# Expert stage of a gated cross-attention block on one core: the next chunk's transpose a unit later, routing squeezed into eight units, and the shared unit written straight to its place

## The reference, cut to what matters

```python
x = x + tanh(g_xattn) * xattn(layernorm(x), ctx, Wq, Wk, Wv, Wo, bo)
h = layernorm(x)
logits = h @ gate_w.T
scores = sigmoid(logits)
choice = scores + bias                     # 4 groups of 8 experts
best two groups by the sum of their best two choices
best 8 experts in these groups; weight = 2.5 * score / sum of the 8 scores
final = sum over experts of weight * down(silu(gate(h)) * up(h))
x = x + tanh(g_ffn) * (final + shared_down(silu(shared_gate(h)) * shared_up(h)))
```

## Time and profile before

| | us |
|---|---|
| median of 3 runs | 726.13 |
| lowest, highest | 724.36, 729.16 |
| the profiled execution, its own time | 733.6 |
| its span, from first to last instruction | 731.8 |
| expert stage in it, from 410 to the end | 322 |
| mean granted TensorE clock | 0.971 |

### The profile page before, as it was taken

How to read it: one execution, slowest core, us unless ns; L and a number is a source line. 1 busy time by engine, 2 the same in 40 slices (tenths; PEclk the granted TensorE clock), 3 DMA queues, 4 the chain that set the end, 5 groups by cost and what they waited for, 6 DMA issues and landing times.

```text
span 731.8 us, 16937 instructions
## 1 busy us (share of the span) xinstructions
PE 701.1 (96%) x4696; PEld 593.8 (81%) x4696; DVE 529.2 (72%) x1646; ACT 333.3 (46%) x626; POOL 268.8 (37%) x317
## 2 busy tenths in 40 slices
PE   8699999999999999999998989999899998999996
PEld 5589898898989889898887867878687786878784
DVE  5556776777767777777746497878778794969663
ACT  3224343343434334443443445556555554555553
POOL 4021212212122121221300165656656563756654
PEclk9859999999999999999997899999999999999999
DMA  5300001000000000000000544435352535454460
GB/s 141 107 19 19 20 20 24 17 17 17 18 23 17 18 17 19 21 17 20 15 2 1 130 105 99 122 95 127 94 140 75 145 100 122 126 119 129 99 150 15
DMA packets 44797, 47.22 MB, mean 65 GB/s; under 512 B 11728, under 2 KB 27216, under 8 KB 44752
## 3 DMA queue, kind: packets, MB, share of 16 engines
q1 hardware_dynamic: 44752, 46.72, 26.0%
HBM read 43.81 MB, written 2.62 MB: 63 GB/s over the span
## 4 chain that ended last, share of the span: by engine, by line
PE 81%; issue 8%; DVE 6%; POOL 3%; DMA 1%; DVEq 1%; POOLq 0%; ACT 0%; SPq 0%; ACTq 0%
PE bank L1052 16%; PE bank L977 11%; PE bank L979 11%; PE bank L978 11%; PE bank L1085 8%; PE bank L1012 5%; PE bank L1060 5%; POOL halves L446 3%; PE bank L1032 3%; PE bank L1038 2%; PE bank L1041 2%; PE bank L1035 2%; PE bank L984 1%; DVE xn L668 1%; PE bank L1022 1%
## 5 line engine op out<-in xcount | busy, mean ns | idle before, releaser
L446 POOL TENSOR_TENSOR halves<-area,halves 128x512 fp32r<-128x512 f32 x136 | 177.0, 1302 | 161.9 <-ACT halves L565 160.9
L522 ACT ACTIVATE area<-bank 128x512 f32<-128x512 f32 x128 | 69.5, 594 | 192.0 <-PE bank L1041 192.0
L937 DVE TENSOR_TENSOR bank<-area,bank 128x512 f32<-128x512 f32 x136 | 93.7, 689 | 62.0 <-PE bank L979 47.9
L1052 PE MATMUL bank<-ctx_keys,area 128*128 128x65 f32 x1024 | 130.1, 281 | 0.0
L1052 PEld LDWEIGHTS bank<-ctx_keys,area 128*128 128x128 f32 x1024 | 127.8, 201 | 0.7 <-issue 0.7
L575 ACT ACTIVATE area<-bank 128x512 f32<-128x512 f32 x136 | 81.3, 598 | 100.7 <-PE bank L979 100.1
L977 PE MATMUL bank<-x2t_hi,w_hi 128*128 128x512 f32 x272 | 110.7, 407 | 3.3 <-DVE area L948 2.4
L979 PE MATMUL bank<-x2t_lo,w_hi 128*128 128x512 f32 x272 | 106.7, 392 | 0.0
L978 PE MATMUL bank<-x2t_hi,w_lo 128*128 128x512 f32 x272 | 106.5, 392 | 0.0
L688 DVE TENSOR_REDUCE row_max<-bank 128x4 f32<-128x512 f32 x128 | 82.2, 684 | 33.5 <-PE bank L1012 32.4
L394 POOL TENSOR_TENSOR ctx_hi<-ctx_raw,ones_col 128x128 fp32r<-128x128 f32 x32 | 12.8, 401 | 253.0 <-PE bank L1041 244.2
(11 more groups left out here) (118 smaller groups left out, 1132.9 us busy)
## 6 DMA issues: line engine op xcount, KB each, us to landing
wbc<-rows_dram SPq DMA_DIRECT2D x128, 256.0 KB, 4.3
w_raw<-experts SPq DMA_DIRECT2D x32, 102.0 KB, 2.0
ctx_raw<-ctx_t SPq DMA_DIRECT2D x64, 32.0 KB, 2.1
out<-area SPq DMA_DIRECT2D x8, 256.0 KB, 3.8
ctx_keys<-ctx_nat SPq DMA_DIRECT2D x32, 32.0 KB, 1.8
max_rows<-max_t SPq DMA_DIRECT2D x64, 4.0 KB
area<-wq_t SPq DMA_DIRECT2D x1, 512.0 KB, 4.2
area<-wo SPq DMA_DIRECT2D x1, 512.0 KB, 4.9
```

The source lines that it names most:

```text
L446: nc.gpsimd.tensor_tensor(hid_lo[:, u % SLOTS, :], hid[:, u % HIDS, :], raw(hid_hi[:, u % SLOTS, :]), ALU.subtract).then_inc(hidlo_ready, 1)
L522: nc.scalar.activation(probs_t[:, k, :, :], st_ps[q][:].rearrange("p (h n) -> p h n", h=4), ACT.Exp)\
L937: nc.vector.tensor_tensor(up_ps[u % UPS][:], silu_g[:, u % 2, :], up_ps[u % UPS][:], ALU.mult)\
L1052: ins = nc.tensor.matmul(u_ps[q][:, i * (CD + 1):(i + 1) * (CD + 1)], probs_t[:, k, i, :], ctx_keys[:, b, :], start=True, stop=True)
```

## The change

Six edits, all in the expert stage:

1. PE: the transposes of chunk c+1 move from behind unit 0 to behind unit 1; the router product moves from behind unit 2 to behind unit 3.
2. ACT: `x2t_out` moves from unit 1 to unit 2, with `x2t_high` right behind it. The Tanh of the logits moves to unit 4, the Silu to unit 5.
3. DVE: step 0 moves from unit 3 to unit 4. Steps 1 to 20 now take 16 places, from place 1 of unit 5 to place 0 of unit 13, where they took 20 places.
4. ACT: `weights_out` moves to the top of unit 15, ahead of that unit's Silu.
5. DVE: in unit 0 `gate_up` writes its product straight into `hid`, and the copy at line 944 goes. For that it now waits until POOL has done the low half of the unit that last used this slot (unit 15 of the chunk before).
6. The counts of the semaphore `gated_ready` are adapted (16 in a chunk, where there were 17).

```diff
-ROUTE_FROM, ROUTE_TO = 4, 14
+ROUTE_FROM, ROUTE_PLACES = 2 * 5 + 1, 16
...
+        def gated_before(c, u):
+            return (UNITS - 1) * c + (u - 2 if u > 0 else 0)
...
             def experts_of(c, parity, first, last):          # ACT
                 for u in range(UNITS):
+                    if u == WEIGHTS_AT + 1 and not last:
+                        weights_out(c + 1)
                     act.wait_ge(gate_done, UNITS * c + u + 1)
-                    wait(act, gated_ready, free_of(2, c, u))
+                    if u == 2:
+                        act.wait_ge(hid_ready, UNITS * c + 1)
+                    else:
+                        wait(act, gated_ready, gated_before(c, u))
...
-                        if u == 1:
+                        if u == 2:
                             x2t_out(c + 1)
-                        if u == 2:
                             x2t_high(c + 1, 1 - parity)
-                        if u == 3:
-                            sigmoids(c + 1)
-                        if u == WEIGHTS_AT + 1:
-                            weights_out(c + 1)
+                        if u == 4:
+                            sigmoid_high(c + 1)
+                        if u == 5:
+                            sigmoid_low(c + 1)
...
-                if u == 3 and place == 1:                    # DVE, levels_at
+                if u == 4 and place == 1:
                     route_levels[0](c + 1)
-                at, places, levels = 2 * (u - ROUTE_FROM) + place, 2 * (ROUTE_TO - ROUTE_FROM), len(route_levels) - 1
+                at, places, levels = 2 * u + place - ROUTE_FROM, ROUTE_PLACES, len(route_levels) - 1
...
-                nc.vector.tensor_tensor(up_ps[u % UPS][:], silu_g[:, u % 2, :], up_ps[u % UPS][:], ALU.mult)\
-                    .then_inc(gated_ready, 1)
+                if u == 0:
+                    wait(dve, hidlo_ready, free_of(HIDS, c, u))
+                    nc.vector.tensor_tensor(hid[:, u % HIDS, :], silu_g[:, u % 2, :], up_ps[u % UPS][:], ALU.mult)\
+                        .then_inc(hid_ready, 1)
+                else:
+                    nc.vector.tensor_tensor(up_ps[u % UPS][:], silu_g[:, u % 2, :], up_ps[u % UPS][:], ALU.mult)\
+                        .then_inc(gated_ready, 1)
...
-                    if u > 0:
+                    if u > 1:
                         weigh_hidden(c, u - 1)
...
-                    if u == 0 and not last:                  # PE
+                    if u == 1 and not last:
                         if not first:
                             pe.wait_ge(wt_ready, c + 1)
                         transpose_norm(NCH + c + 1, misc_ps)
-                    if u == 2 and not last:
+                    if u == 3 and not last:
                         if not first:
                             pe.wait_ge(weight_ready, c + 1)
                         route(c + 1, route_ps)
```

More of the change, by code:

```diff
@@ L490, in x2t_high, with sigmoid_high, sigmoid_low @@
                 nc.scalar.activation(x2t_hi[:, parity, :], x2t[:], ACT.Copy).then_inc(x2hi_ready, 1)
-            def sigmoids(c, ps=route_ps):
+            def sigmoid_high(c, ps=route_ps):
                 act.wait_ge(logits_done, c + 1)
                 nc.scalar.activation(tanh_half[:], ps[:, 0:CB * NE], ACT.Tanh, scale=0.5).then_inc(sig_ready, 1)
+            def sigmoid_low(c, ps=route_ps):
                 act.wait_ge(route_step, ROUTE_STEPS * c + 1)
@@ L545, in attention @@
                     if last and b == 2:
-                        sigmoids(0, scores_ps[1])
+                        sigmoid_high(0, scores_ps[1])
+                        sigmoid_low(0, scores_ps[1])
                     if not (first and b == 0):
@@ L936, in gate_up @@
                 dve.wait_ge(up_done, n + 1)
-                nc.vector.tensor_tensor(up_ps[u % UPS][:], silu_g[:, u % 2, :], up_ps[u % UPS][:], ALU.mult)\
-                    .then_inc(gated_ready, 1)
+                if u == 0:
[5 more added lines that the diff above has]
+                        .then_inc(gated_ready, 1)
             def weigh_hidden(c, u):
-                dve.wait_ge(gated_ready, UNITS * c + u + 1)
+                dve.wait_ge(gated_ready, (UNITS - 1) * c + u)
                 wait(dve, hidlo_ready, free_of(HIDS, c, u))
[L943 to L950, removed]
+                group, i = divmod(u - 1, 2)
+                dve.wait_ge(wbc_in[group % WBC_SLOTS], 32 * (WBC_GROUPS // WBC_SLOTS * c + group // WBC_SLOTS + 1))
+                nc.vector.tensor_tensor(hid[:, u % HIDS, :], up_ps[u % UPS][:], wbc[:, group % WBC_SLOTS, i, :],
+                                        ALU.mult).then_inc(hid_ready, 1)
             def experts_of(c, parity, first, last):
```

## The result

| | before | after |
|---|---|---|
| median | 727.64 (4 runs) | 749.12 (4 runs, 747.78 to 751.75) |
| ratio | | 1.0272, 95% interval 1.0212 to 1.0332 |
| profiled execution, span | 731.8 | 750.0 |
| start of the expert stage (first gate matmul) | 410.07 | 412.28 |
| expert stage, from there to the end | 321.7 | 337.7 |

A forecast was written before the change was run, and what follows sets the result against it. PE, busy 96%, was taken as the bound, with DVE just keeping pace. Terms -7.5 + 11.4 - 0.3 = +3.6 us, less 0.8 for the slow stretch, gave +2.8 on the median 726.13: 728.9, range 718 to 733.

The forecast's parts named there:

- The wait on the normalised chunk: PE's 8.0 us of waits for the next chunk's normalised tiles, chunks 1 to 6; claimed to go, 7.5 us saved net.
- step 2: Routing step on DVE, now in place 0: held behind POOL's low half from 4.76 until 5.93, missing by 0.16 us.
- step 10: Routing copy on DVE: comes at 13.1 while POOL runs from 12.9 to 14.2, so it is held, missing by 0.2 us.
- the sum: DVE and POOL queues added up from unit 5: 1.9 us lost per plain chunk, 11.4 in chunks 1 to 6; total +3.6.
- Step 3's 0.71 us: Routing step on DVE after unit 5's `weigh_hidden`: claimed to meet POOL's `x2t_low` (5.9 to 7.2) and end at 7.28.
- the wait at unit 9: First of PE's waits on `weigh_hidden` claimed before units 9 to 11 in every chunk: 0.28 us of 1.2 a chunk.
- From here the steps are small.: DVE's routing steps after the third added-up wait: claimed to take 0.08 to 0.65 us, so that DVE stays level.
- Step 12: Routing step on DVE that makes the groups' mask: taken at 0.08 us, among the steps assumed small.
- 0.6 us come back there: Chunks 3 and 5: unit 1's up product waits 0.6 us for the old chunk's last `weigh_hidden`, leaving 1.6 saved in each.
- half of it, -0.8: Slow-clock stretch of 1.7 us after chunk 5's idle time: may go with that idle time, so half was counted, -0.8.
- The third one, slower: Rival: step 2 is held by both POOL operations, 2.4 us instead of 1.2; 11 us in all, 737; chance 0.12.
- the first one: Rival: DVE's queue absorbs the denser steps, never more than 1.85 us back; 717 to 718.6; chance 0.20.

The follow-up runs named there:

- packing alone: The kernel before with only the places of the twenty routing steps changed, to 16 places from place 1 of unit 5: ratio 1.0251, median 753.16.
- early copy alone: The kernel before with only the copy of the weights moved to the top of unit 15: ratio 1.0031.
- step 2 from the bank: The changed kernel with routing step 2 reading the logits' bank (PSUM) instead of the SBUF tile: ratio to the kernel before 1.0126.
- copy kept: The changed kernel without the straight product, the shared unit again going through its bank and the copy at line 944: ratio to the kernel before 1.0113.
- step 12 from the bank: The changed kernel with routing step 12, the groups' mask, reading the logits' bank instead of the SBUF tile: ratio to the kernel before 1.0094.
- 18 places: The changed kernel with the twenty routing steps in 18 places, from place 0 of unit 5, instead of 16: ratio to the kernel before 1.0033.
- bank reads: The changed kernel with seven routing steps reading one operand from the logits' bank instead of an SBUF tile: ratio to the kernel before 0.9887, median 724.88.

## Why the prediction was wrong

**Right in kind.** The wait on the normalised chunk went, and VectorE's queue took its place, with steps held behind POOL's subtractions; step 2 and step 10 were held as the sum said, in place 0, by margins of 0.1 to 0.3 us. Step 3's 0.71 us and the wait at unit 9 came as well. But the sum gave +3.6 us for the stage, +2.8 with the slow stretch, and it was +16.0. Four terms were wrong.

**"From here the steps are small."** This failed. Step 12, taken at 0.08 us, takes 0.98: a `tensor_scalar` from SBUF to SBUF, in place 0 of unit 10, and held like step 10, whose 0.16 and 0.57 I had read in the earlier trace rows. I had marked the steps that might be held by the rows in which they were seen held, and this one had stood in place 1 of unit 9. The waits of units 12 and 13 come from it, as its own experiment shows. The other three came as added up: 0.45, 0.37 and 0.45 us, where the sum had 0.28, 0.40 and 0.52. With their restarts the five waits cost 2.7 us a chunk where the three of the sum cost 1.5; the weights, late for their transposes as said, cost 0.4 with the restart. Together that is 3.1 us a chunk instead of 1.9, 18.4 us instead of 11.4. The packing alone has the same: its plain chunk is 3.05 us longer than before.

**The jump: "0.6 us come back there".** This took the idle time of 2.09 us from the trace of before as fixed. Edit 4, which I priced at 0, starts the loads before the jump, and the idle time is 3.83 and some 3.6. The up product of unit 1 waits 2.17 and 1.87 us, by the starts 2.3 and 2.0 later than without it, and 0.1 for each restart: 4.5 us come back in the two chunks and not 1.4. I had looked for who waits for the transfers, and not for whom they are in the way of.

**The slow clock, "half of it, -0.8".** It took the idle time of PE as going; it moved, and both chunks now have a slow stretch: +1.8 us.

**Edit 5, priced at 0.** It brings the small wait at the top of every second chunk, 1.1 us in all, whose cause stays open.

Together, with chunk 0 at -0.8 where the sum had -0.3: -8.9 of removed waits + 4.5 + 18.4 + 1.8 + 1.1 - 0.8 = 16.1, against 16.0 measured. The 16.0 us of the stage are 2.2% of the whole; the timed ratio holds more than that. The four timed runs of the changed kernel all had mean clocks of 0.968 to 0.973, and those of the kernel before lie between 724.36 and 736.06 us. How much of the 2.7% comes from the front, 4 runs against 4 can't tell.

**The rivals.** The third one, slower, was the nearest in size, and for the wrong reason: step 2 got in between POOL's two subtractions (1.35 us, not 2.4). The time that the first one gives, in which the queue takes it, is about that of the kernel that leaves routing alone and of the one whose steps read a bank (0.988 and 0.989).

## What to carry to other kernels

Before small operations of VectorE are moved or packed beside a busy GpSimd, mark every one that reads only SBUF (two tiles, or one in a copy or `tensor_scalar`), and not just those that were seen held: a place is cheap or dear by where GpSimd stands in the unit, not by the operation's own length (step 12: 0.16 us or 0.98). A transfer that starts earlier can lengthen an engine's idle time behind a loop's jump (3.83 us for 2.09), so its start belongs behind the jump. And of a change in several parts, the part that removes the wait is worth a run of its own: here it brought 1.2%, and the packing beside it cost more than twice that.

## What the runs showed that I had not expected

An idle time of PE costs more than the profile prints beside it: 0.29 us shown, 0.45 from start to start, and 0.1 for the restart. VectorE loses 2.1 us at most jumps back in this loop (2.05 to 2.44), and 2.8 to 3.8 when broadcast loads of 256 KB are already running. At the top of chunks 3 and 5 PE had nine waits of 1.75 to 3.26 us (in the kernel before, the changed one, packing alone, early copy alone and once with step 2 from the bank). In or behind eight of them the granted clock fell to its lower level, 0.50; each such stretch cost 1.7 us, and one 3.4. It fell behind none of the nine of 1.18 to 1.69 us there (the other one with step 2 from the bank, and those with the copy kept, step 12 from the bank, 18 places and bank reads).
